# Layernorm of the first layer's graph product: from matmuls over features on partitions to VectorE statistics over nodes on partitions

## The reference, cut to what is computed

```python
h = relu(adj @ x @ gcn_w + gcn_b)                      # 4096 x 128
mu, var = h.mean(-1), h.var(-1)
h = (h - mu) * rsqrt(var + 1e-5) * ln_g + ln_b
xz = h @ w_in                                          # 4096 x 512: xc | z
u = silu(causal_conv4(xc) + conv_b)
dbc = u @ w_xp; dt = softplus(dbc[:, :8] @ w_dt + b_dt); B, C = ...
state = exp(dt*A) * state + dt*B*u;  ys = state @ C     # scan over the 4096 nodes
out = ((ys + u*D_skip) * silu(z)) @ w_out
x1 = layernorm(x + out)
# second layer: MLP1(adj @ x1), MLP2(adj @ x2), merged by Wm
result = layernorm(x1 + concat(MLP1, MLP2) @ Wm.T + bm)
```

## Time and profile before

| what | value |
|---|---|
| median of 3 runs | 822.98 us (821.73 to 824.44) |
| the profiled execution | 822.56 us, span 820.8 us |
| mean granted clock of TensorE | 0.998 |
| TensorE busy | 805.8 us (98%), 2080 instructions |
| GpSimd busy | 659.6 us (80%) |
| VectorE busy | 600.1 us (73%) |
| ScalarE busy | 377.5 us (46%) |
| HBM traffic | 277 GB/s over the span |

### The profile page before, as it was taken

How to read it: one execution, slowest core, us unless ns; L and a number is a source line. 1 busy time by engine, 2 the same in 40 slices (tenths; PEclk the granted TensorE clock), 3 DMA queues, 4 the chain that set the end, 5 groups by cost and what they waited for, 6 DMA issues and landing times.

```text
span 820.8 us, 7303 instructions
## 1 busy us (share of the span) xinstructions
PE 805.8 (98%) x2080; PEld 365.4 (45%) x2080; DVE 600.1 (73%) x800; ACT 377.5 (46%) x615; POOL 659.6 (80%) x318
## 2 busy tenths in 40 slices
PE   7999999999999999999999999999999999999996
PEld 3434444444454444444444444444444454444453
DVE  0025998699878887898799878887988789782135
ACT  0045475357535644466356534653456455231234
POOL 2007999999999899899999999889998999960036
PEclk9999999999999999999999999999999999999999
DMA  9979867666765999999689976889867896797602
GB/s 340 408 269 378 258 241 256 224 245 211 255 211 186 351 361 338 353 357 334 232 277 332 370 254 204 284 289 375 300 228 281 303 347 219 269 331 263 253 26 78
DMA packets 62957, 227.61 MB, mean 277 GB/s; under 512 B 7346, under 2 KB 8004, under 8 KB 44356
## 3 DMA queue, kind: packets, MB, share of 16 engines
q1 hardware_dynamic: 24228, 156.33, 51.1%
q10 hardware_dynamic: 38688, 70.80, 26.6%
HBM read 224.48 MB, written 2.62 MB: 277 GB/s over the span
## 4 chain that ended last, share of the span: by engine, by line
PE 94%; DVE 2%; DMA 1%; ACT 1%; issue 0%; SPq 0%; DVEq 0%
PE p_x L481 52%; PE p_x L504 16%; PE p_two L504 11%; PE p_m L593 2%; PE p_dA L668 2%; PE p_m L577 2%; DMA ring<-adj_blocks 1%; PE p_two L567 1%; PE p_m L560 1%; PE p_m L597 1%; PE p_m L531 1%; PE p_m L537 1%; PE p_h L668 1%; PE p_m L542 1%; PE p_m L534 1%; PE p_two L547 1%
## 5 line engine op out<-in xcount | busy, mean ns | idle before, releaser
L481 PE MATMUL p_x<-ring,x_s 128*128 128x512 f32 x1024 | 457.8, 595 | 3.7 <-DMA ring<-adj_blocks 2.1
L1107 POOL TENSOR_TENSOR y<-y,prod 128x1024 f32<-128x1024 f32 x127 | 300.0, 2363 | 29.6 <-DVE prod L924 29.0
L481 PEld LDWEIGHTS p_x<-ring,x_s 128*128 128x128 f32 x1024 | 193.0, 191 | 251.2 <-issue 246.7
L1098 POOL TENSOR_TENSOR bh<-spread,dtu 128x1024 f32<-128x1024 f32 x128 | 302.6, 2365 | 0.1
L915 DVE TENSOR_TENSOR_SCAN p_h<-p_dA,state,bh 128x512 f32<-128x512 f32 x224 | 276.2, 1279 | 31.9 <-ACT p_dA L678 22.9
L678 ACT ACTIVATE p_dA<-dt,A 128x512 f32<-128x512 f32 x256 | 170.5, 686 | 104.6 <-DVE p_h L915 103.7
L924 DVE TENSOR_TENSOR prod<-p_h,spread_C 128x1024 f32<-128x1024 f32 x128 | 155.4, 1214 | 0.0
L504 PE MATMUL p_x<-ring,x 128*128 128x512 f32 x304 | 137.3, 593 | 0.0
L504 PE MATMUL p_two<-ring,x 128*128 128x512 f32 x208 | 94.5, 593 | 0.5 <-DVE dt L974 0.5
L504 PEld LDWEIGHTS p_x<-ring,x 128*128 128x128 f32 x304 | 57.4, 190 | 72.7 <-issue 72.7
L411 POOL TENSOR_SCALAR dtu<-prod,mv,rstd 128x128 f32<-128x128 f32 x26 | 20.3, 794 | 65.7 <-ACT rstd L902 65.7
(11 more groups left out here) (125 smaller groups left out, 582.4 us busy)
## 6 DMA issues: line engine op xcount, KB each, us to landing
ring<-adj_blocks SPq DMA_DIRECT2D x144, 1024.0 KB, 7.3
spread<-bc_rows ACTq DMA_DIRECT2D x128, 256.0 KB, 5.1
spread_C<-bc_rows ACTq DMA_DIRECT2D x128, 256.0 KB, 6.1
x_s<-x_tiles SPq DMA_DIRECT2D x8, 256.0 KB, 7.4
x_s<-x_tiles ACTq DMA_DIRECT2D x7, 256.0 KB, 13.8
out_tiles<-dtu SPq DMA_DIRECT2D x7, 256.0 KB, 2.1
pack<-pack_w ACTq DMA_DIRECT2D x1, 1026.5 KB, 25.8
ring<-adj_blocks SPq DMA_DIRECT2D x4, 256.0 KB, 5.7
```

What stands on the lines that cost most here:

```text
L481: return pe.matmul(bank[:, :], tiles[:, JT * m + jt, :], ring[:, i % RING, jt, :], start=opens, stop=closes)
L1098: pool.tensor_tensor(bh[:, i % 3, :, :], both(spread[:, i % SLOTS, :]), dtu[:, c % 2, :, :], ALU.mult).then_inc(s_bmul, 1)
L1107: pool.tensor_tensor(y[:, c % 2, :, :], y[:, c % 2, :, :], prod[:, i % 2, :, :], ALU.add).then_inc(s_acc, 1)
```

## The change

Nodes go on partitions for the layernorm. `gcn` becomes four matmuls of 128x128, each with a slice of `ax` as the stationary operand and `gcn_w` as the moving one, so that `p_m4[:, t, :]` holds 128 nodes by 128 features. VectorE then adds the bias (broadcast, `gb`), applies relu, takes `bn_stats` and `bn_aggr` over the free dimension and negates the mean. ScalarE computes 1/sqrt(var + eps) and the shift and normalises in place. VectorE transposes in 32x32 blocks (`transpose`, 128x512), and ScalarE puts the 16 blocks where they belong in `hr`, 16 copies of 32 partitions by 4x32 elements, which completes the 128x128 transposes. From `in_x` on all is as before.

```diff
-FILL = {"gcn": 0, "cen": 1, "var": 3, "in_x": 7, "x_proj": 3, "dt": 18}
+FILL = {"gcn": 12, "in_x": 7, "x_proj": 3, "dt": 10}
...
-        at = tuple(2 * origin(c) + q - (c == 0) for q in (-1, 1, 2, 4, 9, 12))
-        for name, q in zip(("gcn", "cen", "var", "in_x", "x_proj", "dt"), at):
+        at = tuple(2 * origin(c) + q - (c == 0) for q in (-1, 5, 9, 12))
+        for name, q in zip(("gcn", "in_x", "x_proj", "dt"), at):
...
-                    pe.matmul(p_m[:, :], gcn_w, ax[:, n % 2, :], start=True, stop=True).then_inc(s_gcn, 1)
-                elif name == "cen":
-                    pe.wait_ge(s_hr, n + 1)
-                    pe.matmul(p_m[:, :], cen_w[:, :], hr[:, :], start=True, stop=True).then_inc(s_cen, 1)
-                elif name == "var":
-                    pe.wait_ge(s_sq, n + 1)
-                    pe.matmul(p_m[:, :], mean_w[:, :], sq[:, :], start=True, stop=True).then_inc(s_var, 1)
+                    for t in range(JT):
+                        last = pe.matmul(p_m4[:, t, :], ax[:, n % 2, P * t:P * (t + 1)], gcn_w, start=True, stop=True)
+                    last.then_inc(s_gcn, 1)
...
+                if name == "norm":
+                    act.wait_ge(s_hst, 3 * n + 3)
+                    act.activation(rstd[:, 2 + b, :], mv[:, 2 + b, :, 1], ACT.Ln, bias=eps_t[:, :]).then_inc(s_hrs, 1)
+                    act.wait_ge(s_hrs, 3 * n + 1)
+                    act.activation(rstd[:, 2 + b, :], rstd[:, 2 + b, :], ACT.Exp, scale=-0.5).then_inc(s_hrs, 1)
+                    act.wait_ge(s_hrs, 3 * n + 2)
+                    for t in range(JT):
+                        last = act.activation(shift_h[:, t:t + 1], nmean_h[:, t:t + 1], ACT.Copy,
+                                              scale=rstd[:, 2 + b, t:t + 1])
+                    last.then_inc(s_hrs, 1)
+                    act.wait_ge(s_hrs, 3 * n + 3)
+                    for t in range(JT):
+                        last = act.activation(sq4[:, t, :], sq4[:, t, :], ACT.Identity,
+                                              bias=shift_h[:, t:t + 1], scale=rstd[:, 2 + b, t:t + 1])
+                    last.then_inc(s_norm, 1)
+                elif name == "moves":
+                    act.wait_ge(s_turn, n + 1)
+                    wait(act, s_z, G * n)
+                    for q in range(P // Q):
+                        for r in range(P // Q):
+                            last = act.activation(hr4[Q * r:Q * (r + 1), :, Q * q:Q * (q + 1)],
+                                                  turned[Q * q:Q * (q + 1), :, Q * r:Q * (r + 1)], ACT.Copy)
+                    last.then_inc(s_h, 1)
...
-                if name == "var":
-                    dve.wait_ge(s_rs, n + 1)
-                    dve.tensor_tensor(hr[:, :], hr[:, :], p_m[:, :], ALU.mult).then_inc(s_h, 1)
+                if name == "stats":
+                    dve.wait_ge(s_gcn, n + 1)
+                    if n == 0:
+                        dve.wait_ge(s_consts_in, 64)
+                    dve.tensor_tensor(sq4, p_m4, gb_tiles, ALU.add).then_inc(s_gb, 1)
+                    dve.wait_ge(s_gb, n + 1)
+                    dve.tensor_scalar(sq[:, :], sq[:, :], 0.0, None, ALU.max).then_inc(s_relu, 1)
+                    dve.wait_ge(s_relu, n + 1)
+                    for t in range(JT):
+                        last = dve.bn_stats(bn6[:, t, :], sq4[:, t, :])
+                    last.then_inc(s_hst, 1)
+                    dve.wait_ge(s_hst, 3 * n + 1)
+                    for t in range(JT):
+                        last = dve.bn_aggr(mv[:, 2 + b, t, :], bn6[:, t, :])
+                    last.then_inc(s_hst, 1)
+                    dve.wait_ge(s_hst, 3 * n + 2)
+                    dve.tensor_scalar(nmean_h[:, :], mv[:, 2 + b, :, 0], -1.0, None, ALU.mult).then_inc(s_hst, 1)
+                elif name == "turn":
+                    dve.wait_ge(s_norm, n + 1)
+                    wait(dve, s_h, n)
+                    dve.transpose(turned[:, :, :].rearrange("p t n -> p (t n)"), sq[:, :]).then_inc(s_turn, 1)
```

82 lines of the change are left out of this document (32 added, 50 removed).

## The result

The changed kernel takes **826.59 us** (median of 20 executions), the kernel before beside it 822.82. Two of the 20 lie far off (1447 us, at a mean granted clock of 0.62, and 2175 us); the median of the other 18 is 826.2, and the ratio is of them. The ratio is 1.0036, with a 95% interval of 1.0020 to 1.0052: slower by a third of a percent, about 3 us. The prediction was 822.0 us, a gain of 0.8, and "nearly all of the gain is given back in chunk 0". A loss came instead: the forecast was 4.6 us too low. The 18 executions of the changed kernel lie from 822.2 to 833.1 us where those of the kernel before lie from 821.7 to 824.4. The experiments show two places that cost about equally: two small instructions on VectorE that wait for GpSimd, and the 16 copies on ScalarE. Taking the waits away, or cutting the copies from 5.1 to 0.9 us, saves some 10 us each.

A forecast was written before the change was run, and what follows sets the result against it. TensorE, busy 98% of the span, was taken to bound the kernel. Terms -15.2 + 0.4 + 8.3 + 1.4 + 0.3 + 4.0 = -0.8 us gave 821.8 (profiled) or 822.2 (median); forecast 822.0 us, range 813.5 to 833.5.

The forecast's parts named there:

- Removed from TensorE: All chunks: cen and var products 13.7 us, w_in fold 1.0, ax wait 0.8, less 0.3 for gcn: 15.2 us less.
- The copies: ScalarE's 16 copies into hr: spacing 0.21 us from back-to-back activations, 16 x 0.21 + 0.09 = 3.5 us.
- Rival 1: Copies run 0.39 us apart like L797: 12.6 us more, 834 us; decides from about 0.25 spacing; chance 0.12.
- Relu and mean: VectorE's statistics step: 3.6 + w, w being relu's wait for GpSimd, 0 to 2.3 us; on average 4.7 us.
- rival 4: Relu and mean wait little or nothing: 3.1 us less in chunk 0, 4.0 in others, 0.3 clock; 814.6 us; chance 0.20.
- The other pieces of the chain: Between gcn and in_x: ScalarE's norm 3.1 us, covered while shorter than 3.9, and VectorE's transpose 0.69 us.
- Prologue: Start: in_x at 49.65 us instead of 46.14, TensorE waits 0.4, scans start 3.7 later, z at 73.7.
- Chunk 0: hr at 107.7 us; TensorE waits 8.3 up to in_x (3.5 at the next row's first product), 1.4 at x_proj.
- Clock: TensorE slowed after idle stretches of 3.5 and 4.8 us in chunk 0: 0.3 us, bounds 0 and 4.
- Chunks 1 to 6: No wait at in_x (hr at z + 29.1, TensorE at z + 30.1); 0.7 us a chunk at x_proj, 4.0 for six.
- the prediction's own sign: The prediction is wrong if in_x waits in later chunks too, or if chunk 0 shows no wait.
- 7 us of slack at `out`: Chunks 1 to 6: GpSimd loses 0.4 us a chunk to relu and has 7 us of slack at out.

The follow-up runs named there:

- cut_two: The kernel before with the centring and variance products cut from 512 columns to 4, every wait and other instruction kept: 813.26 us.
- nomean: The changed kernel with relu reading PSUM instead of SBUF and the negative mean made by a copy on ScalarE instead of VectorE: 816.84 us.
- late0: The changed kernel with chunk 1's in_x, x_proj and dt products three half units later in TensorE's order in chunk 0: 824.13 us.
- nomean_late: nomean with the in_x, x_proj and dt products in chunk 0 two half units later on TensorE: 819.78 us.
- nm_take_late: nomean_late with ScalarE's copy of the finished row 1 out of p_x put ahead of unit 1's decays: 816.71 us.
- after_nm: The changed kernel with only the negative mean moved to ScalarE, relu still from SBUF to SBUF: 820.95 us.
- copies4: The changed kernel with the 16 copies replaced by 4 of 128 x 128 without change of partitions, so h is not the transposed one: 816.24 us.
- nm_all_late: nm_take_late with in_x, x_proj and dt of the chunks behind also one half unit later on TensorE: 822.72 us.
- b_pro: The kernel before with 8 extra 128 x 512 copies on ScalarE ahead of in_x's first copy in the prologue: 830.45 us.
- b_pro2: b_pro with 11 of TensorE's products behind dt moved ahead of x_proj to keep TensorE covered: 826.89 us.

## Why the prediction was wrong, step by step

What failed is the length of the chain from `gcn` to `hr`, in two of its terms: the copies (3.5 us, measured 5.1) and the bound on relu's wait w (2.3 us, measured 4.2 in chunk 0), with a slowed clock behind the longer wait (0.3 us, measured 2.7). The place was forecast rightly. z(1) came 6.0 us later than the 158.5 of the prediction, 1.8 of them already at z(0); from z(1) to the last product with y the kernel then won 4.8 us on the kernel before, where 5.3 had been forecast. The forecast for that execution was 821.8, and it took 828.24. How the miss splits between the copies, w and the clock is open: the copies and the waits were only taken away, never set to their predicted size, and the clock was never changed by itself.

- **Removed from TensorE, 15.2 us.** Busy time fell by 9.9 us, 2.7 of passes at half speed and other longer ones included. In cut_two five sixths of such a cut arrive at the end. The 0.8 us at `gcn` of the prologue went as said.
- **The copies, 16 x 0.21 = 3.5 us.** The row was of activations on 128 partitions. Those overlap, the copies of 32 partitions do not: 0.318 us apart, 5.1 us. `hr` for chunk 1 was ready 4.4 us later than the forecast 107.7, and about 3 us of that is this term, once in the prologue (the scans start later by it) and once in chunk 0. Rival 1 had named the risk. The point "about 0.25" from which it was to decide was passed, and its price was too high: 12.6 us for a spacing of 0.39.
- **Relu and mean, 3.6 + w.** The rule behind it was right as far as it goes: both end with an instruction of GpSimd when it runs. First, w is not bounded by one instruction: in chunk 0 relu waited for two (4.60 us), so the step took 6.8 us instead of 5.8, 1.0 of the 4.4 us. In chunk 1 it was issued at 183.11, 0.24 us before GpSimd's instruction ended, and still waited for the next (2.83 us); in chunks 2, 4 and 5, with 0.24 or 0.25 us left, it got in (0.52 or 0.53 us). Second, the mean waited 0.7 us three times and not at all in chunks 0, 1, 3 and 6, because GpSimd, starved meanwhile, was idle. So in chunks 1 to 6 the step took 3.8 us on average, less than the 4.7 taken. Third, the price: nomean shows that both waits together cost 9.8 us at the end, more than rival 4 gave them (7.4, the distance from 822.0 to 814.6).
- **The other pieces of the chain.** Norm 3.1 us and transpose 0.69 measured as taken.
- **Prologue.** `in_x` came at 51.41 instead of 49.65, of which 1.6 us are the copies. TensorE waited 0.48 us there (0.4 predicted), and 0.84 us for a block of the ring that had not been foreseen; z(0) began at 75.53 instead of 73.7. The scans began 5.2 us later than before instead of 3.7.
- **Chunk 0.** The first product of the next row waited 2.93 us (3.5). `hr` was there at 112.15 instead of 107.7: 1.7 us from the scans, which started 1.5 us later than forecast, 1.0 from relu, 1.6 from the copies, 0.2 around them. TensorE came to `in_x` 29.2 us after z(0), that wait included, as predicted (25.7 and 3.5). The waits sum to 10.45 us instead of 8.3.
- **Clock.** 0.3 us was predicted with bounds 0 and 4; it was 2.7. The reason given, that what is slowed stands ahead of a wait at `x_proj`, fell with that wait: `x_proj` did not wait (1.4 predicted), as VectorE and ScalarE kept pace there.
- **Chunks 1 to 6.** "No wait" at `in_x` was wrong in chunk 1 (2.56 us) and chunk 3 (1.61), right in the others; by the prediction's own sign this shows it wrong. The margin there was 1.0 us (29.1 against 30.1), and the 1.6 us of the copies alone are more than that. From z(1) to z(7) the kernel won 3.6 us on the kernel before, where 10.3 us of products less 4.0 had been 6.3.
- **GpSimd.** "7 us of slack at `out`" was read from chunk 2. In chunk 0 there is none to spare: after the late start GpSimd starved for 3.12, 1.87 and 1.25 us and took 89.8 us from its first product of the chunk to the gate where it took 83.5. late0, nomean_late and nm_take_late, which are 4.0 to 4.5 us ahead of nomean at z(1) and 1.4 to 3.2 behind it at z(2), speak for this chain, not TensorE, setting the end of chunks 0 and 1.

## What to carry to other kernels

Price an instruction by what it may wait for, not by its elements: 128 x 4 elements waited as long as 512 columns here. The wait went when relu read PSUM and when the mean was made on ScalarE. A spacing read from instructions on 128 partitions need not hold for 32. Before work is moved off the busiest engine, see how much room the second busiest has in the fullest stage, and test it with a short dummy: 1.5 us a chunk were free, 5.7 were not. A wait of TensorE that is filled by a later place in its order is only moved when another engine's chain ends at the same time.

## What was new on the hardware

- A waiting instruction of VectorE can be passed by GpSimd's next one, and place alone does not tell when. Over the four kernels with relu from SBUF to SBUF (changed, after_nm, copies4, late0), relu was issued 0.26 us or less before the end of GpSimd's instruction 17 times: it got in 15 times and was passed twice (2.83 us, and 2.69 in after_nm). With 2.0 us left in chunk 0 it was passed in the changed kernel (4.60 us) and not in copies4 and late0 (2.29 and 2.30). So the traced execution of the changed kernel holds two unlucky cases, in chunks 0 and 1; how many its median execution holds is not known.
- Whether this makes the spread of the changed kernel's executions (11 us) is not shown, and two kernels speak against it as the only cause: nm_all_late, with both such instructions gone, spreads over 7.5 us, and copies4, with both in it, over 2.9.
- VectorE's max on 512 columns takes 0.43 us from SBUF and 0.69 us from PSUM, and the slower form was the better one beside a busy GpSimd.
- Copies on ScalarE of 128 partitions overlap (0.206 us apart at 0.29 us each), copies of 32 partitions don't (0.318 us apart at 0.307 each).
- After a wait of 7.5 us TensorE ran its next passes at 1.2 GHz (granted clock 0.50), after the wait of 4.9 us in b_pro as well, and after those of 3.03 us in b_pro2 and 2.45 in nomean_late some of them. After waits of 2.93 and 2.56 us in the changed kernel the granted clock stayed at 1.00.
